# A gated-delta-rule layer between two recurrent FFNs: state steps begun after the first FFN instead of beside its last two blocks

## The reference

```
x = x + 0.5 * ffn(layernorm(x));  x = x + attn(layernorm(x));  x = x + 0.5 * ffn(layernorm(x))

ffn(x), for x of [8, 1024, 256]:            # a scan over the first axis, 8 steps
    c = in_c
    for xt in x:
        f, i = sigmoid(xt wf' + c uf' + bf), sigmoid(xt wi' + c ui' + bi)
        c = f * c + i * tanh(xt wc' + c uc' + bc)
    return tanh(x wo' + c uo' + bo)
attn(x):                                    # 16 heads of 16 features
    s = x W';  k = q = rmsnorm(x per head) * k_norm_w;  v = -s
    over the 1024 tokens, per sequence and head:
        S = lam * S;  S += beta * k (v - k S);  o = q S
    return layernorm(s + o) * o_norm_w + o_norm_b
```

## Time and profile before

| | us |
|---|---|
| median of 3 runs (1555.32 to 1564.24) | 1555.78 |
| the profiled execution's own time | 1562.62 |
| its span, from the first to the last instruction | 1560.8 |
| TensorE, VectorE, ScalarE, GpSimd busy | 1380.0, 924.6, 689.2, 197.3 |

### The profile page before, as it was taken

One profiled execution on the slowest core, in us unless ns is written; L12 is line 12 of the kernel. 1 busy time (PEld: TensorE's weight loads), 2 busy tenths in 40 slices (PEclk: granted clock), 3 DMA queues, 4 the chain that ended last, 5 costly groups with the idle time before them and its releaser, 6 DMA issues.

```text
span 1560.8 us, 61982 instructions
## 1 busy us (share of the span) xinstructions
PE 1380.0 (88%) x27811; PEld 1277.7 (82%) x27811; DVE 924.6 (59%) x2208; ACT 689.2 (44%) x1585; POOL 197.3 (13%) x230
## 2 busy tenths in 40 slices
PE   4889899998989899888888988889899999999887
PEld 4878798888979788777877887878788989898776
DVE  2646686777867766558655774664444645554532
ACT  2253454545445444443444444344445445444332
POOL 0001010010100100002400320040130404040400
PEclk9999999998999989998889979989999999999999
DMA  4011112112211323232224222421534333332000
GB/s 128 1 41 68 42 44 84 58 75 67 78 63 58 124 64 95 91 119 65 73 82 131 68 90 64 158 70 47 166 88 119 98 110 107 90 122 80 28 28 28
DMA packets 64201, 125.39 MB, mean 80 GB/s; under 512 B 12352, under 2 KB 33088, under 8 KB 61888
## 3 DMA queue, kind: packets, MB, share of 16 engines
q1 hardware_dynamic: 63936, 121.43, 24.3%
HBM read 62.13 MB, written 59.24 MB: 78 GB/s over the span
## 4 chain that ended last, share of the span: by engine, by line
PE 61%; DVE 21%; issue 9%; ACT 7%; DVEq 0%; ACTq 0%
PE ps L426 29%; PE ps L493 7%; PE ps L1007 6%; PE ps L818 4%; PE ps L642 4%; PE ps L991 4%; DVE ln_bn L83 3%; ACT gates L443 3%; PE ps L667 2%; ACT ffn_rows L101 2%; DVE ig L469 2%; PE ps L386 1%; ACT gates L450 1%; PE ps L478 1%; DVE prod L743 1%
## 5 line engine op out<-in xcount | busy, mean ns | idle before, releaser
L426 PE MATMUL ps<-cst,wt 128*128 128x128 f32 x2688 | 360.7, 290 | 8.3 <-DVE cst L471 7.8
L426 PEld LDWEIGHTS ps<-cst,wt 128*128 128x128 f32 x2688 | 331.3, 201 | 20.0 <-DVE cst L471 9.1
L426 PE MATMUL ps<-ffn_rows,wt 128*128 128x128 f32 x2304 | 300.3, 288 | 17.4 <-DVE hs L506 6.4
L426 PEld LDWEIGHTS ps<-ffn_rows,wt 128*128 128x128 f32 x2304 | 285.7, 203 | 25.9 <-issue 15.8
L465 DVE TENSOR_TENSOR fc<-gates,cst 128x256 f32<-128x256 f32 x112 | 51.7, 461 | 285.0 <-ACT gates L443 284.9
L443 ACT ACTIVATE gates<-ps,colv 128x128 f32<-128x128 f32 x448 | 127.1, 365 | 173.9 <-PE ps L426 173.6
L1007 PE MATMUL ps<-e,kgb 32*128 32x64 f32 x4032 | 129.6, 275 | 7.9 <-issue 4.1
L1007 PEld LDWEIGHTS ps<-e,kgb 32*128 32x128 f32 x4032 | 120.6, 189 | 16.6 <-issue 10.6
L1096 POOL TENSOR_TENSOR ffn_rows<-ffn_rows,rowv 128x256 f32<-128x256 f32 x64 | 54.3, 882 | 573.5 <-DMA ffn_rows<-x_scratch 573.5
L818 PE MATMUL ps<-inv_cols,kv 32*32 32x32 f32 x8192 | 92.4, 201 | 34.3 <-DVE zbd L1037 17.4
L618 POOL TENSOR_TENSOR kg_rows<-key_rows,g_tok 128x512 f32<-128x512 f32 x32 | 46.4, 1478 | 594.9 <-DVE key_rows L581 594.9
(11 more groups left out here) (117 smaller groups left out, 1793.5 us busy)
## 6 DMA issues: line engine op xcount, KB each, us to landing
kg_scratch<-kg_rows SPq DMA_DIRECT2D x32, 512.0 KB, 3.9
xs_scratch<-xs_out SPq DMA_DIRECT2D x32, 512.0 KB, 3.6
xsb<-xs_scratch SPq DMA_DIRECT2D x64, 256.0 KB, 3.5
kgb<-kg_scratch SPq DMA_DIRECT2D x256, 64.0 KB, 2.6
ffn_rows<-x SPq DMA_DIRECT2D x32, 256.0 KB, 3.4
x_scratch<-ffn_rows SPq DMA_DIRECT2D x32, 256.0 KB, 2.7
e_scratch<-e SPq DMA_DIRECT2D x256, 32.0 KB, 1.7
ffn_rows<-e_scratch SPq DMA_DIRECT2D x8, 1024.0 KB, 6.2
```

The source lines that it names most:

```text
L426: mm = pe.matmul(banks[g][:, col:col + P], wt[:, w, k, m * P:(m + 1) * P], rhs, start=(x in (0, FI)), stop=(k == KT - 1 and (t == 0 or x > ...
```

## The change

`SOLO` goes from 6 to 8, so `JOIN` is 64, `FIRST_HOP` 65, and `SECOND` is `JOIN` + 16 = 80. All eight blocks of `ff` run in the `first_*` functions. Sixteen steps follow without an FFN: hops 0 to 14 with the pieces due at the blocks 8 and 9. From step 80 the second FFN runs beside hops 15 to 63; its first block still has the last four units (`ta4` to `ta7` of block 7), as block 10 had. In the steps without an FFN part 0 is issued between states and update on TensorE, and ahead of the state copies on ScalarE and VectorE. Post stages stay 8 steps behind their hops. The last step is 146, not 130. The load of x1 for the first two posts moves from a step's t of 1 to t of 2, into `transfers`.

```diff
-SOLO = 6
+SOLO = NB
-SECOND = TILE * NB
+SECOND = JOIN + 2 * TILE
@@ fill_table
     for i in range(JOIN, END):
         b, t = divmod(i, TILE)
-        n = b - NB
...
+        n = b - SECOND // TILE
+        if t == 0 and 0 <= n < NB:
+            singles((2,), *four("fr2", n, (2, 3)))
+        if n < 0:
+            for behind, name in PERIOD[t][0]:
+                piece(name, b - behind)
         if hop_at(i) is not None:
             last_hop = hop_at(i)
             ahead_of_hop[last_hop] = list(counts)
...
@@ transfers
+            if t == 2 and prep.real and not prep.ahead(2).real:
+                sp.wait_ge(ln2.applied, 8 * (prep.n + 1))
+                sp.wait_ge(x_out[prep.p], prep.quarters_landed)
+                sp.dma_start(xt[prep.p], x1_d[prep.n + 2 - NB]).then_inc(x1_in[prep.p], 16)
@@ first_pe (first_act has the same for act_front)
-                ff.pe_front(pe, b.ahead(1), (0, 1))
+                if b.ahead(1).real:
+                    ff.pe_front(pe, b.ahead(1), (0, 1))
@@ second_pe
                 if s is not None:
                     hop_states_pe(pe, s)
...
+                if b is None:
+                    pieces(pe, *period_of(i, 0), prep_pe, solve_pe)
+                else:
+                    fg.pe_step(pe, b, t, *((0, NX) if t == 0 else (NX, NX + FI)))
+                    if t == 0:
+                        fg.pe_front(pe, b, (3,))
                 if s is not None:
                     hop_update_pe(pe, s)
...
+                if b is not None:
+                    if t > 0:
+                        fg.pe_step(pe, b, t, NX + FI, 2 * NX)
+                    if t < 7:
+                        fg.pe_step(pe, b, t + 1, 0, FI)
+                    pieces(pe, *period_of(i, 0), prep_pe, solve_pe)
...
                 pieces(pe, *period_of(i, 1), prep_pe, solve_pe)
@@ second_act
                 if s is not None:
                     hop_act(act, s)
                 post_act(act, i, 0)
...
+                if b is None:
+                    pieces(act, *period_of(i, 0), prep_act, solve_act)
+                else:
...
                 if s is not None:
                     state_act(act, s)
...
-                    if i == SECOND - 1:
-                        act.wait_ge(ff.h_full, 4 * (NB - 1) + 2)
...
+                        if nxt.n == 0:
+                            act.wait_ge(ff.h_full, 4 * NB)
+                        if nxt.n == 1:
+                            act.wait_ge(kg_out, 64 * NB)
+                        fg.act_front(act, nxt, (0, 1))
@@ second_dve
+                if b is not None:
+                    fg.dve_step(dve, b, t, (0,))
+                else:
+                    pieces(dve, *period_of(i, 0), prep_dve, solve_dve)
                 if s is not None:
                     state_dve(dve, s)
...
                 post_dve(dve, i)
...
+                pieces(dve, *period_of(i, 1), prep_dve, solve_dve)
```

More of the change, by code:

```diff
@@ L228, in fill_table @@
             ahead_of_hop[last_hop] = list(counts)
-        for behind, name in PERIOD[t][0] + PERIOD[t][1] + (LAST_GRAM if t == TILE - 1 else []):
+        if n >= 0:
+            for behind, name in PERIOD[t][0]:
+                piece(name, b - behind)
+        for behind, name in PERIOD[t][1]:
             piece(name, b - behind)
         if t == TILE - 1:
-            if n + 1 < NB:
-                singles((4, 5), *four(*(("fr1", b + 1) if n + 1 < 0 else ("fr2", n + 1)), (0, 1)))
+            for behind, name in LAST_GRAM:
+                piece(name, b - behind)
+            if 0 <= n + 1 < NB:
+                singles((4, 5), *four("fr2", n + 1, (0, 1)))
             for behind, name in LAST_UNIT:
                 piece(name, b - behind)
-            if n < NB:
-                singles((2,), ("ct1", b) if n < 0 else ("ct2", n))
+            if 0 <= n < NB:
+                singles((2,), ("ct2", n))
     return table, behind_hop, ahead_of_hop
@@ L1105, in step_of @@
         def step_of(i):
[L1107 to L1110, removed]
+            b, t = divmod(i - SECOND, TILE)
+            return (Block(b), t) if 0 <= b < NB else (None, t)
         def ending(i):
[L1114 to L1117, removed]
+            b, t = divmod(i - SECOND, TILE)
+            return Block(b - 1) if t == 0 and 1 <= b <= NB else None
         def starting(i):
-            f, b, t = step_of(i + 1)
-            return (f, b) if f is not None and t == 0 else (None, None)
+            b, t = step_of(i + 1)
+            return b if b is not None and t == 0 else None
         def period_of(i, part):
@@ L1129, in second_pe @@
             for i in range(JOIN, END):
-                f, b, t = step_of(i)
+                b, t = step_of(i)
                 s = hop_at(i)
-                old, done = ending(i)
-                new, nxt = starting(i)
+                done, nxt = ending(i), starting(i)
                 if s is not None:
                     hop_states_pe(pe, s)
[L1136 to L1146, removed]
+                if done is not None:
+                    fg.pe_h(pe, done, 2)
+                if b is not None and t == 0:
+                    fg.pe_front(pe, b, (2,))
+                if done is not None:
+                    fg.pe_h(pe, done, 3)
@@ L1153, in second_pe @@
[L1153 to L1156, removed]
-                    f.pe_h(pe, b, 0)
+                if b is not None:
[4 more added lines that the diff above has]
+                    pieces(pe, *period_of(i, 0), prep_pe, solve_pe)
+                    if t < 7:
+                        fg.pe_step(pe, b, t + 1, FI, NX)
+                    else:
+                        fg.pe_h(pe, b, 0)
@@ L1273, in second_sp @@
                         load_kg(sp, s + 2)
-                prep = Block(b - 1)
                 transfers(sp, Block(b), t)
-                if t == 1 and prep.real and not prep.ahead(2).real:
-                    sp.wait_ge(ln2.applied, 8 * (prep.n + 1))
-                    sp.wait_ge(x_out[prep.p], prep.quarters_landed)
-                    sp.dma_start(xt[prep.p], x1_d[prep.n + 2 - NB]).then_inc(x1_in[prep.p], 16)
-                n = b - 1 - NB
+                n = b - 1 - SECOND // TILE
                 if t == 1 and n >= 0:
```

94 lines of the change are left out of this document (39 added, 55 removed).

## The result

The changed kernel takes 1601.91 us in the median (1600.15 to 1604.11, four runs), the kernel before 1559.35 on the same chip (1555.32 to 1564.24, four runs). The ratio is 1.0272 (95% interval 1.0231 to 1.0313): slower by 2.7%, where 1566, 0.6% above before, had been forecast, with a range of 1532 to 1592. The changed kernel's profiled execution took 1603.58, with a span of 1601.8, and is read here against the sum of 1350.8 + 220 = 1570.8.

The account below looks back on a forecast made before the run. TensorE was taken to set the pace where all three kinds of work meet. Terms 720.2 + 80.8 + 410 + 139.8 = 1350.8 plus 220 for X gave a span of 1570.8, 1566 as median; range 1532 to 1592.

Parts of the forecast that it names:

- blocks 6 and 7: Last two blocks of the first FFN: without state steps they take 95.0 us each, 190 together.
- the plain blocks: Second FFN beside state steps alone: five blocks, where three were, at 82.0 us each, 410 together.
- The tail: Last two blocks and the ending, from 1421.0 on: unchanged at 139.8 us.
- the intervals: Sixteen steps without an FFN, from one step's state copies to the next's, 14 in all: 167.5 us at full clock.
- Term (d): Second FFN's block 0, with state steps, a post stage and four units: 80.8 us.
- X: First FFN's last `cst` to second FFN's first, sixteen steps without an FFN: 206.5 to 233 us, 220 taken.
- the walk: Step-by-step pricing of the sixteen steps without an FFN at full clock: 28 + 167.5 + 11 = 206.5 us.
- the FFN's time simply leaves: Rival, sixteen steps without an FFN: cover not lost, 165 us in place of 279.3, 1530 in all; chance 0.20.
- The clock: Sixteen steps without an FFN: half rate after TensorE idles adds 26 us if it holds throughout; the middle taken.
- The ends of X: Before and after the 14 intervals: 28 us to the first state copies, 11 to the second FFN's first `cst`.
- the floor: Instruction supply in the sixteen steps: 3.8 us per 256 instructions on TensorE, binding single intervals, 19 in step 72.
- the second rival: Sixteen steps: TensorE idling holds the clock at 1.2 GHz, 233 or 243 us there, 1579 to 1589 overall; chance 0.37.

## Why the prediction was wrong, point by point

**What held.** The redistribution: blocks 6 and 7 came down to 95.1 and 93.8, and the plain blocks stayed at 82.3 on average. The tail is the same to 0.1. No wait for a load of x1 is among TensorE's long ones in the intervals. Term (d) was 6.8 too high: in its model, 1094.2 to 1175.0, TensorE had stopped 7.9 for instructions (5.2 ahead of units, 2.7 ahead of states), and here 2.4 in the same matmuls, which is 5.5 of it. I had taken one block's stops for a fixed price. The chain in X is also the one described: free banks take 46.5 out of it, and at full clock its first six intervals came within 6 of the walk (in the kernel with idle matmuls). The rival "the FFN's time simply leaves" is refuted: it needed 165 where the trace has 261.0. The code's own waits, the reason given against it, are not the whole of that, since with free banks it is still 214.5.

**The step that failed** is the paragraph "The clock": "Priced by that row (half as much again for units, grams, states and update ...) the half rate adds 26 if it holds throughout" and "I take the middle, 220". It was mis-sized twice.

First, how much of the longer work lies on the path. The paragraph charges 24 to the 14 intervals for the half rate throughout, "some 1.5 in most others". Its own factors give more. On the walk's TensorE work, half as much again for updates, states, units and grams is 34, and up to twice for v products (7.3) and eleven groups of transposes (12) another 20: up to 54 in all, and the trace has 53. So the factors were right as a sum, and over half of the excess was taken to vanish in waits. It didn't: the intervals took 47 more than the walk. Step 74, at half clock from end to end, shows it. The walk has 10.8 for it and 1.5 for the clock. Two units, eight transposes, the update and the states would be 4.0 by the factors, 14.8 with the walk. The trace has 16.0, with TensorE busy for 11.83 where the full-clock prices make 6.9:

```profile
873.10:889.10 16.00, 11.83 (x392) 10.73 (x392) 8.28 (x16) 2.85 (x4) 0.00 (x0) 0.50 0.18 45
```

Of the two steps that were charged nothing because VectorE is last, 69 took 13.6 for 10.2 at a clock of 0.63, and 79 the 9.1 of the walk at 0.50.

The factors themselves depend on the form. Measured at 0.50: update 3.69 for 2.01 (1.84 times), states 1.94 for 1.18 (1.64), a unit 1.93 for 1.29 (1.5), a gram 2.04 for 1.48 (1.38), eight transposes 1.97 for 1.14 (1.7). Only the unit is what "half as much again" said. The update, the one group that every step has on its path, has the largest: 0.7 more than at 1.5 times, in every step at half clock. Transposes and v products (11.1 for 7.3, at a clock that was low for a part of them) made up for it by staying under "twice". The trace of before had the update's price: the only one near the window of the earlier trace rows takes 2.60 from 927.04 on, and the clock rose at 928.3, so that row has both rates in it; 1.26 us at 3.69 for the whole and the rest at 2.01 make 2.6.

Second, how long it holds. I argued that v products and grams could lift the clock again and took half. It did rise during the v products of steps 67 and 68, and stayed up for what followed directly. Timeline of after, the v products of step 67 and its update at full rate:

```profile
770.72 5.69 PE L652 MATMUL ps<-wt,key_cols 128*128 128x256 f32 x16
777.13 2.01 PE L1022 MATMUL ps<-e,kgb 32*128 32x64 f32 x64 [0.72 <-issue]
```

It didn't last: the states of step 69 take 1.94 again. With the grams it didn't rise: from 829.4 to 969.3 it stayed at 0.50, through three of the four grams and nine units, with 63% of TensorE's time busy (87.6 of 139.9). Before that, from 746.7 on, it came and went, and the first six intervals took 88.7 with 0.65 granted, against 72.7 with 0.97 in the kernel with idle matmuls. That a clock at the slow level is the state that only steady work leaves, as the Trainium skill has it (page "TensorE: Matmul & The Clock Gate", Part 1: The HAM clock gate), agrees with this trace as a whole: 0.56 over the intervals.

By my prices the half rate throughout made X = 233. Measured it is 206.5 with 47 more in the intervals, 3 in the start and 4.5 in the end: 261. For the first six intervals, 22 over the walk, the kernel with idle matmuls shows that about 16 is the clock's; for the other eight it is read from the longer TensorE groups alone.

**The ends of X.** The end of 15.5 for 11 is the same cause: TensorE was busy for 15.32 of it at 0.73, and the kernel with idle matmuls took 12.0 at 1.00. The start's 3.2 are gone with free banks (27.6), at the same clock, so they are mostly the bank order in step 65.

**Step 75.** I charged 4 for solve operations beside GpSimd's additions. They took 0.6 each, and GpSimd has no instruction near them. The interval was 19.3, not 21.0; VectorE is last in it, as said. Timeline of VectorE and TensorE of after there:

```profile
897.27 0.62 DVE L756 TENSOR_TENSOR inv<-inv,prod 128x448 f32<-128x448 f32 x1
...
901.75 1.07 DVE L770 TENSOR_SCALAR xs_out<-ps,w_x 128x512 f32<-128x512 f32 x1
...
903.18 3.69 PE L1022 MATMUL ps<-e,kgb 32*128 32x64 f32 x64 [9.80 <-DVE xs_out L770]
```

TensorE idles 9.80 for the solve, and then runs the update at half rate.

**The instructions.** I held "if everywhere on top of the half rate it gains 10" open. The gain isn't seen in what could be tested. Stops of TensorE that issue ended come to 14.5 in the intervals, in pieces of up to 2.1, but with three grams of step 72 cut to an eighth the interval gave back their own work and two stops, no more. So the floor did not bind the step with most instructions, and some stops lie on the path; how many of the others do is open. The Trainium skill (page "Runtime: NRT & Kernel Launch", Instruction fetch mechanics) calls the cost of crossing from one piece of the stream to the next mostly hidden. If the stops here are such crossings, this case agrees only in part: 2.1 us of them were given back in one step.

**The rivals.** The result is the second rival, "the clock stays down", with its place and its mechanism (chance 0.37), but at 18 over even its upper price of 243. The mechanism stood there and was underpriced. That it weighed so much because the banks made the chain serial fits the groups (47 of 53 on the path) and the kernel with free banks, whose intervals took 171.9 with the same long updates and units, only 4 over the walk at full clock.

**What stays open.** What the clock alone costs in this kernel wasn't isolated, since every way tried to hold it adds work: some 16 in six intervals is shown, by one trace of each kernel; the 47 for all is the difference to a walk, set beside group totals. Nor was it tried what the change would cost with free banks and the clock up without added work.

## What to carry to other kernels

A serial chain whose waits were covered by dense work is not freed by taking that work away: count what the chain's banks or buffers share with side work, and give the side work its own (46.5 of 261.0 here) before moving anything. Price a possible low clock per form of instruction, from rows that lie inside the low window, add it in full wherever the chain is serial (here 47 of 53 lay on the path), and give a real chance to its holding throughout (here from 829.4 to 969.3 without a break). The best version found is half of the move with banks of its own for the pieces: ratio 0.9964 (0.9949 to 0.9980), while the whole move with its own banks only comes back to about the time before (1.0029).

## What was not expected of the hardware

With free banks TensorE was busy for 77% of the intervals (132.46 of 171.90) and was granted 0.58. With idle 128x256 matmuls in between it was busy for 84% (168.03 of 200.10) and granted 0.84, and in the FFN's blocks it is busy for 92% at 0.95. Single intervals go the other way round. Step 70 with free banks, and step 66 with idle matmuls in shared banks:

```profile
787.30:799.40 12.10, 11.58 (x306) 10.59 (x296) 5.75 (x5) 4.26 (x7) 8.66 (x10) 0.50 0.21 57
```
```profile
743.40:756.50 13.10, 11.34 (x413) 9.64 (x412) 8.16 (x16) 7.92 (x14) 0.00 (x0) 1.00 0.31 94
```

Busy for 96% at half clock, and for 87% at full clock. A part of the first share is the half clock's own work, since the same matmuls are busy for longer at it. So a busy share alone did not tell the granted clock here; what does was not tried. The cost of the low level differs by form from 1.38 to 1.84 times. And a stop of TensorE for instructions can reach 3.37 in the middle of a unit, as in this row of the kernel with idle matmuls (what it cost there was not measured):

```profile
847.94 0.39 PE L828 MATMUL ps<-inv_cols,kv 32*32 32x32 f32 x24 [3.37 <-issue]
```
